# A two-layer GNN on one core: cell, picks and scatters streamed together, and a message stage with table offsets and types one group later

## The reference

```python
h = relu(layernorm(x))                                  # x: 12500 x 128
msg = h[src] @ W_msg.T + b_msg + edge_embed[type]       # 212500 edges, sorted by dst
m = segment_sum(msg, dst)                               # 12500 x 128
x = x + gru_cell(m, h, W_ih, W_hh, b_ih, b_hh)
h = relu(layernorm(x))
agg = segment_sum(h[dst], src)                          # layer 1: rows src, columns dst
z = ((1 + eps) * h + agg) @ W1.T + b1
z = relu(batchnorm(z, gamma, beta))                     # statistics over all nodes
x = x + z @ W2.T + b2
```

## Time and profile before

| what | value |
|---|---|
| runs | 5644.68, 5648.10, 5653.43 us; median 5648.1 us |
| profiled execution | 5650.5 us, its span 5648.7 us |
| mean granted TensorE clock | 0.644 |
| busy share of the span | PE 57%, PEld 46%, DVE 47%, ACT 28%, POOL 59% |
| DMA | 514 MB, 91 GB/s over the span |

### The profile page before, as it was taken

How to read it: one execution, slowest core, us unless ns; L and a number is a source line. 1 busy time by engine, 2 the same in 40 slices (tenths; PEclk the granted TensorE clock), 3 DMA queues, 4 the chain that set the end, 5 groups by cost and what they waited for, 6 DMA issues and landing times.

```text
span 5648.7 us, 78171 instructions
## 1 busy us (share of the span) xinstructions
PE 3221.0 (57%) x17495; PEld 2607.6 (46%) x17496; DVE 2670.9 (47%) x4799; ACT 1608.2 (28%) x3266; POOL 3336.2 (59%) x3510
## 2 busy tenths in 40 slices
PE   4566666666666665665943333333335666666767
PEld 3344444444444444444733222322324565556656
DVE  7566665666665656664641011111003444445557
ACT  4323222222222322222432222222222222221137
POOL 0666666666666666665136666666666666655563
PEclk8555555555555555555975555555556888878889
DMA  4222222222222111111222222222223444445455
GB/s 144 79 69 67 68 66 68 67 67 67 69 68 66 54 44 43 44 44 39 65 74 74 71 71 74 74 71 74 70 71 128 159 161 146 154 152 174 175 186 181
DMA packets 311629, 514.05 MB, mean 91 GB/s; under 512 B 68678, under 2 KB 227065, under 8 KB 295517
## 3 DMA queue, kind: packets, MB, share of 16 engines
q0 software_dynamic: 106944, 226.05, 13.4%
q1 hardware_dynamic: 118669, 242.40, 13.0%
q10 hardware_dynamic: 85904, 44.17, 2.6%
HBM read 331.72 MB, written 180.64 MB: 91 GB/s over the span
## 4 chain that ended last, share of the span: by engine, by line
another core or an unknown queue 33%; PE 25%; issue 20%; DVE 9%; ACT 5%; ACTq 2%; DVEq 2%; POOL 1%; DMA 1%; SPq 0%; POOLq 0%
PE ps L1700 6%; PE ps L1715 6%; PE ps L1569 4%; PE ps L1583 3%; PE ps L1591 2%; DVE sb_Y L1356 2%; ACT sb_counts L740 2%; DVE sb_blks L1157 2%; PE ps L1739 2%; ACT sb_ring L852 1%; ACTq L848 1%; PE ps L1712 1%; DVEq L1165 1%; DVE sb_oh L1146 1%
## 5 line engine op out<-in xcount | busy, mean ns | idle before, releaser
L649 POOL DMA_INDIRECT rows_by_src<-sb_ring,sb_posE x1664 | 1631.5, 980 | 966.1 <-ACT sb_ring L852 485.3
L626 POOL DMA_INDIRECT sb_ring<-msg_table,sb_stepE x1664 | 1576.9, 948 | 1034.6 <-SPq L466 498.6
L1700 PE MATMUL ps<-sb_H,sb_oh 128*128 x3520 | 725.0, 367 | 1161.9 <-issue 517.6
L1700 PEld LDWEIGHTS ps<-sb_H,sb_oh 128*128 128x128 f32 x3520 | 620.3, 263 | 1265.6 <-issue 1263.8
L1569 PE MATMUL ps<-sb_ring,sb_oh 128*128 x3520 | 926.9, 435 | 216.8 <-issue 208.4
L1569 PEld LDWEIGHTS ps<-sb_ring,sb_oh 128*128 128x128 f32 x3520 | 779.0, 319 | 310.0 <-issue 306.0
L1338 DVE TENSOR_SCALAR sb_oh<-sb_oh,sb_cf 128x512 f32<-128x512 bf16 x440 | 215.4, 503 | 1212.4 <-remote 933.9
L852 ACT COPY sb_ring<-ps 128x512 f32<-128x512 f32 x416 | 242.8, 584 | 1913.0 <-remote 1308.1
L740 ACT CAST sb_counts<-ps 54x512 bf16<-54x512 f32 x440 | 254.8, 579 | 1757.3 <-remote 1198.7
L1189 DVE TENSOR_TENSOR sb_Y<-sb_Y,ps 128x512 f32 x440 | 300.0, 682 | 636.6 <-remote 576.6
L1583 PE MATMUL ps<-sb_oh,sb_toh 128*54 128x128 bf16 x1760 | 320.0, 301 | 261.2 <-issue 252.3
(11 more groups left out here) (225 smaller groups left out, 3855.2 us busy)
## 6 DMA issues: line engine op xcount, KB each, us to landing
sb_stepE<-rows_by_src SPq DMA_DIRECT2D x114, 1088.0 KB
sb_oh<-step_targets SPq DMA_DIRECT2D x110, 512.0 KB
rows_by_src<-sb_cf ACTq DMA_DIRECT2D x294, 136.0 KB
sb_ring<-msg_table,sb_stepE POOLq DMA_INDIRECT x1664
rows_by_src<-sb_ring,sb_posE POOLq DMA_INDIRECT x1664
sb_ring<-rows_by_src SPq DMA_DIRECT2D x11, 1088.0 KB, 5.1
msg_table<-sb_oh SPq DMA_DIRECT2D x14, 448.0 KB, 3.2
sb_oh<-in_x SPq DMA_DIRECT2D x49, 128.0 KB, 2.1
```

The costliest lines, as they stand in the source:

```text
L626: pool.indirect_dma_start(out=ring[:, m % RGROUPS * G + q, 0:F], out_offset=None, in_=table_d[:, :], in_offset=bass.IndirectOffsetOnAxis(a ...
L649: pool.indirect_dma_start(out=rows_d[:, :], out_offset=bass.IndirectOffsetOnAxis(ap=posE[:, m * G + q:m * G + q + 1], axis=0), in_=ring[:, ...
L1700: m = mm(picked_ps[:, ds(slot, P)], pick[g][:, q * P:(q + 1) * P], H[:, ds(off, P)], start=False, stop=True, skip_group_check=True)
```

## The change

- Every block boundary gets a step without edges of its own: `STEPS` is 1856, `CHUNKS` 116, `GROUPS` 464; tiles and their number stay.
- Message stage: PE takes a step's place in its bank from a table row (`relrow`) instead of subtracting, and the number of tile groups needed from the same register (`wait_group`) instead of a load for each group. `add_types` of group n-1 stands behind the ranks of group n, and DVE's add too is one group later.
- The cell is unrolled; POOL's add moves to DVE; x1 goes to 8 small buffers, and ACT normalizes each turn's two blocks from there, with the deviations taken in 13 portions (`LN_ENDS`). Within the same turns the first 56 step groups (`STREAMED` = 7 pairs) are picked, copied and scattered, from turn 6 on. The separate stage of norms is gone.
- Picks use 2 banks instead of 4. A pick of group n waits until groups 0 to n-1 are copied and cleared (`bank_clear` >= n+2). ACT copies once per step group (464) to a place from a table (a spare place where no tile group ends) instead of once per tile group (416).
- POOL tells ACT which ring places are free (`ring_free`, after the DMAs of tile group m-2 have landed). SP relays `row_slot`. The DMAs that load rows for the sums and most of those for the targets are issued by ACT instead of SP.
- The compares of picks (after the streamed ones) and of sums read their constant from PSUM; a pick's `tensor_scalar` becomes a `tensor_tensor`.

```diff
-STEPS = E // P + BLOCKS
+STEPS = E // P + 2 * BLOCKS
+XB1, XSEMS = 8, 4
+LN_ENDS = (1, 3) + tuple(range(7, TURNS - 1, 4)) + (TURNS - 1,)
+STREAMED = -(-TURNS // (2 * GPC))
+SLOT_LAG = 2
...
+        def norm_lag(t):
+            return 6 if t < LN_ENDS[1] + 1 else 8
...
@@ POOL @@
             def scatter(m):
-                pool.wait_ge(S("row_moved"), m + 1)
+                if m >= SLOT_LAG:
+                    f = m - SLOT_LAG
+                    pool.wait_ge(S(f"ring_dma{f % RGROUPS}"), GATHERED + (f // RGROUPS + 1) * (G * 16))
+                    nc.gpsimd.sem_inc(S("ring_free"), G)
+                if m < AHEAD:
+                    pool.wait_ge(S("row_slot"), pool.value_load(endrow[:, m:m + 1], min_val=1, max_val=GROUPS))
+                else:
+                    pool.wait_ge(S("row_moved"), m - AHEAD + 1)
...
@@ ACT @@
+            def move_rows(n, g):
+                src = act.snap(place_regs[g], min_val=0, max_val=512)
+                dst = act.snap(place_regs[GPC + g], min_val=0, max_val=TRASH)
+                key = act.value_load(slot_keys[:, ds(n, 1)], min_val=1, max_val=TILES - G + 1)
+                rows = ring_steps[:, ds(dst, G * RW)].rearrange("p (q w) -> p q w", w=RW)
+                act.wait_ge(S("ring_free"), key)
+                nc.scalar.copy(rows[:, :, KEY:KEY + 1], key_cols[:, ds(key, G)].unsqueeze(2))
+                act.wait_ge(S("picked"), n + 1)
+                nc.scalar.copy(rows[:, :, 0:F], picks_f[:, ds(src, 512)].rearrange("p (q f) -> p q f", f=F)) \
+                    .then_inc(S("row_slot"), 1)
+                act.wait_ge(S("row_slot"), n + 1)
+                nc.scalar.copy(picks_f[:, ds(src, 512)], zeros_b[:, :]).then_inc(S("bank_clear"), 1)
...
+            for i in range(streamed + 10):
+                for n in (n for n in range(streamed) if n + norm_lag(n) + 2 == i):
+                    move_rows(n, n % GPC)
+                if i < TURNS:
+                    gates(i)
+                if i + 2 < TURNS:
+                    move_msg(i + 2)
+                if 1 <= i <= TURNS:
+                    candidate(i - 1)
+                if i - 4 in LN_ENDS:
+                    deviation1(i - 4)
+                for t in (t for t in range(TURNS) if t + norm_lag(t) == i):
+                    norm1(t)
...
@@ DVE @@
             step_blocks(first_d, bstep_d, blktmp)
+            step_blocks(first_m1, bnext_d, blktmp)
...
                         dve.wait_ge(S("y_zero"), 1)
-                    dve.wait_ge(S("agg_done"), n + 1)
-                    wait(dve, "agg_added", n)
-                    yb = Y[:, ds(offs[g], 512)]
-                    vs.tensor_tensor(yb, yb, bank(1 + g), ALU.add).then_inc(S("agg_added"), 1)
+                    else:
+                        add_group(n - 1, (g - 1) % G, off_sets[k if g else 1 - k][(g - 1) % G])
...
+            def stream(i):
...
+                if blend:
+                    dve.wait_ge(S("zhn_ready"), i)
+                    vs.tensor_tensor(hnbuf[o], hnbuf[o], nbuf[o], ALU.add).then_inc(S("hn_ready"), 1)
+                for n in (n for n in range(2 * GPC * STREAMED) if n + norm_lag(n) == i):
+                    layer1_pick(n // (2 * GPC), n // GPC % 2, n % GPC)
...
+                o = vs.tensor_scalar(pick[g], codes, row, None, ALU.is_equal) if row is iota_p \
+                    else vs.tensor_tensor(pick[g], codes, row.to_broadcast([P, 512]), ALU.is_equal)
...
-                                 iota_f.unsqueeze(1).to_broadcast([P, G, P]), ALU.is_equal).then_inc(S("key_oh_v"), 1)
+                                 key_iota.unsqueeze(1).to_broadcast([P, G, P]), ALU.is_equal).then_inc(S("key_oh_v"), 1)
...
@@ PE @@
+            def wait_group(g):
+                pe.reg_alu(need, regs[g * G], 1, ALU.max)
+                pe.wait_ge(S("tiles_in"), pe.snap(need, min_val=1, max_val=TGROUPS))
...
-                    o = bank(1 + g)[:, 0:P] if q == 0 else ps[:, 1 + g, ds(rel(g, q), P)]
+                    o = bank(1 + g)[:, 0:P] if q == 0 else ps[:, 1 + g, ds(place(s), P)]
...
+                    if not isinstance(n, int) or n > 0:
+                        add_types((g - 1) % G, n - 1)
                     pe.wait_ge(S("agg_zero"), n + 1)
-                    wait_tiles("tiles_in", n)
+                    wait_group(g)
                     sum_rows(g, k, n)
-                    add_types(g, n)
...
+            picked_ps = ps[:, 6:8, :].rearrange("p a b -> p (a b)")
+            def pick_group(n, g):
+                pe.wait_ge(S("bank_clear"), n + 2)
+                pe.wait_ge(S("pick_oh"), n + 1)
+                for q in range(G):
+                    off = pe.snap(regs[g * G + q], min_val=0, max_val=(BLOCKS - 1) * P)
+                    slot = pe.snap(slots[g * G + q], min_val=0, max_val=(2 * G - 1) * P)
+                    m = mm(picked_ps[:, ds(slot, P)], pick[g][:, q * P:(q + 1) * P], H[:, ds(off, P)],
+                           start=False, stop=True, skip_group_check=True)
+                m.then_inc(S("picked"), 1)
+            for i in range(streamed + 9):
+                if i < TURNS:
+                    gates(i)
+                if i + 2 < TURNS:
+                    msgT(i + 2)
+                if 2 <= i < TURNS + 2:
+                    back(i - 2)
+                for n in (n for n in range(streamed) if n + norm_lag(n) + 1 == i):
+                    pe.wait_ge(S("h2_norm"), min(n + 1, TURNS))
+                    pick_group(n, n % GPC)
```

More of the change, by code:

```diff
@@ L550, in _, with relay_rows @@
-            pick_loop(sp, feed)
+            for i in range(TURNS):
+                x1_out(i)
+                if i + 2 < TURNS:
+                    cell_in(i + 2, i % 2)
+                if i % GPC == 2 and i >= 10:
+                    c = (i - 10) // GPC
+                    sp.wait_ge(S("pick_oh"), (c + 1) * GPC)
+                    loc_in(sp, c + 2, c % 2)
+            def relay_rows(m, r):
+                last = sp.value_load(endrow[:, ds(m, 1)], min_val=1, max_val=GROUPS + 1)
+                sp.wait_ge(S("row_slot"), last)
+                nc.sync.sem_inc(S("row_moved"), 1)
@@ new lines, in norm1 @@
+            def norm1(i):
+                act.wait_ge(S("ln_ready"), sum(i > e for e in LN_ENDS) + 1)
+                for b in range(NG):
+                    n = i * NG + b
+                    o = nc.scalar.activation(H[:, n * P:(n + 1) * P], x1buf[i % XB1][:, b * P:(b + 1) * P], ACT.Relu,
+                                             bias=nbn[:, n:n + 1], scale=rstdn[:, n:n + 1])
+                o.then_inc(S("h2_norm"), 1)
+            place_regs = [act.alloc_register(f"slot_place{q}") for q in range(2 * GPC)]
@@ L857, in _ @@
-            act.wait_ge(S("ring_tails"), 1)
-            for g in range(GPC):
-                clear_picks(g).then_inc(S("bank_clear"), 1)
-            for r in range(RGROUPS):
-                move_rows(0, r)
-            with act.Fori(1, TGROUPS // RGROUPS) as j:
-                for r in range(RGROUPS):
-                    move_rows(j, r)
+                move_msg(k)
+            for g in range(2):
+                nc.scalar.copy(bank(6 + g), zeros_b[:, :]).then_inc(S("bank_clear"), 1)
+            streamed = 2 * GPC * STREAMED
@@ new lines, in _, with srows_in, slots_and_feed @@
+            act.wait_ge(S("x1_kept"), TURNS)
+            def srows_in(s, k):
+                act.dma_start(srows[k].rearrange("p a w -> p (a w)"), rows_of(s)) \
+                    .then_inc(S(f"rows_in{k}"), 16)
+            def slots_and_feed(j, k, sums, first, own):
+                c = j * 2 + k
+                if first in FIRST_C:
+                    z = FIRST_C.index(first)
+                    landed(act, z)
+                    for s, h in ((first, first % 2), (first + 1, 1 - first % 2)):
+                        wait(act, "sum_done", (s - 1) * GPC)
+                        srows_in(s, h)
+                slot_regs(c)
+                for g in range(GPC):
+                    move_rows(c * GPC + g, g)
+                    if g == GPC - 1 and not (isinstance(c, int) and c + 2 >= CHUNKS):
+                        loc_in(act, c + 2, k)
+                    for i, (s, h) in enumerate(sums):
+                        if (i * GPC + GPC - 1) // len(sums) == g:
+                            after = [FIRST_C[z + 1] for z in range(NPASS - 1) if isinstance(s, int) and s < FIRST_C[z + 1]]
+                            if not (isinstance(s, int) and s + 2 >= after[0]):
+                                act.wait_ge(S("sum_done"), (s + 1) * GPC)
+                                srows_in(s + 2, h)
@@ L1313, in norm_relu @@
[L1313 to L1325 removed]
+                        m = vs.bn_aggr(v[:, 2 * b:2 * b + 2], stats[:, b * 6:(b + 1) * 6])
```

484 lines of the change are left out of this document (246 added, 238 removed).

## The result

The kernel after takes 5733.15 us (median of 3 runs, 5730.66 to 5743.51) against 5648.1: ratio 1.0162, 95% interval 1.0145 to 1.0178. It is slower; the forecast was 5480 us.

What follows compares the result with a forecast made beforehand. No engine was taken as saturated: stages wait, with the ledger on POOL's queue. Terms 4 - 70 - 163 + 60 = -169 took 5650.5 to 5481 profiled, so 5480 us; range 5280 to 5740.

Steps and rivals of the forecast that it cites:

- the scatters' term: Scatters on POOL's queue: 2627 us against 2567, +60, with waits of 48 in streamed turns and 485 in later picks.
- and the old 1.6 with sums, where PE's sums fill the time: Picks with sums: POOL's wait per tile group stays at 1.6 us, 264 us in all.
- The message term: Message stage: PE's shorter work lets 2.5 step groups finish per ring refill, 186 waits, -70 us.
- next late is DVE: Message stage: PE's wait for ACT's copy goes; DVE, whose ranks PE needs, is late next. No size given.
- The bound of +27: Message stage, slow end: still 2.04 step groups per refill, 227 waits of 2.31 us, 525 us, +27.
- The gap: Between last gather and first scatter: 233.3 us falls to 70, -163.
- Streamed turns: Cell turns that also pick and scatter: 5.4 us each, 56 turns, 302 us for 50 tile groups.
- Rival A: Picks and streamed turns: held PE increments make the kernel slower, 5845 us at worst; chance 0.23.
- Constants in PSUM: Compares reading constants from PSUM shorten POOL's indirect DMAs: half of the 35 us excess, -18.
- 5740 with two of the three: Total if two of three prices hold: message 97, streamed turns +118, picks without sums +150.
- a drained POOL ends each hold, so waits limit themselves: Argument against the held-increments rival: late increments arrive once POOL has run dry. No size given.
- B: Whole kernel: POOL becomes the bound and the ring never runs dry, 5040 us, likelier 5260; chance 0.17.

Runs made afterwards that it cites:

- e8b: Repeat of the kernel after with four pick banks behind the streamed groups, early types and constants in SBUF; late (slower) chip: 5578.8 us, ratio 1.0002 to the kernel before.
- a2: The kernel after, unchanged, on a late (slower) chip: 5654.2 us, ratio 1.0133 to the kernel before.
- e6: The kernel after with types and adds back in their own step group, table offsets kept; late (slower) chip: 5647.3 us, ratio 1.0115 to the kernel before.
- e7: Both kernels with a lag between PE's picks and ACT's copy; late (slower) chips: before 5635.1 and 5626.0 us, after 5745.4 and 5752.0.
- e2: The kernel after with the compares' constants back in SBUF, on a prompt (faster) chip: 4739.0 us, ratio 0.9896 to the kernel before.
- e5: The kernel before with scatters as direct writes of a tile to a fixed place; late (slower) chip: 5018.7 us, one run.
- e8: The kernel after with four pick banks behind the streamed groups, early types and constants in SBUF; late (slower) chip: 5583.0 us, ratio 0.9994 to the kernel before.
- e3c: The kernel before with a pick waiting as if there were two banks, one tile group allowed uncopied; late (slower) chip: 5603.1 us, ratio 1.003.
- e1: The kernel before with only the order changed, types and adds one group later; prompt (faster) chip: 4789.5 us, ratio 0.9998.
- a0: The kernel after, unchanged, on a prompt (faster) chip: 4716.1 us, ratio 0.9848 to the kernel before.

## Why the prediction was wrong

- **The failed step: the scatters' term (+60, measured +225).** POOL's own time came out at 1614.6 + 463.9 us, 15 under the forecast's 2094. The waits are the error: 714 us against 48 + 485. By the waits in the three windows: streamed turns 107 us, forecast 48; without sums 244, forecast 221; with sums 364, forecast 264. More than half of the excess of 181 lies where the chain got no price, and the step that failed in words was "and the old 1.6 with sums, where PE's sums fill the time". It was 364/165 = 2.2 us per tile group there, since the strict chain runs beside the sums too (with slack behind the picks, e8b, POOL's waits for copies there were 299 us against 343 in a2); without sums, where I had priced the chain, 244/201 = 1.2 against 1.1.
- **The message term (-70, measured +27).** The wait for ACT's counts went and "next late is DVE" came true (L350's 422 us for L1275), but the term rested on PE's shorter work filling the ring faster, and that step failed too, by 97 us: POOL was refilled once in 464/209 = 2.2 groups, not 2.5, and waited longer each time (2.50 us for 2.31). The bound of +27 was hit to the microsecond, though by luck: it was reckoned from added groups, and in e6 and e7 these cost nothing and the later types about 27. On prompt chips there is no wait to win (2085 and 2086 us).
- **The gap (-163, measured -179)** had its reason right, on either kind of chip (-165): the first copy came 33 us after the cell's start, forecast 36. The rest is mostly an earlier start, 19 us after the last gather instead of 33.5.
- **Streamed turns (302 us, measured 367).** On a prompt chip they take 316 (5.6 us per turn), and the late increments add 51. The 5.4 was 4.6 of summed work and 0.8 for held increments. A prompt chip has no holds and still needs 5.6, so the sum of ACT's and POOL's times was 1.0 too low and the price came near by luck. Rival A's 7.5 us a turn was too much.
- **Constants in PSUM (-18).** POOL's scatters fell from 1631.5 to 1614.6 us, -17, but the half that I took was luck. The excess of mean over median went from 21 to 1 ns, nearly all of the 35 us and not half of it. The median rose from 959 to 969 ns, 17 us, for a reason that no run shows; e2 has the 969 too. And the 690 ns that the prediction sets beside what is said of PSUM operands belong to a compare that reads SBUF alone (L1346), so they don't show it; a pick's compare with an operand in PSUM takes 684 (L1428) where it took 503.
- **Rivals.** A had the mechanism and the sign, with 0.23 against the forecast's 0.45. That "5740 with two of the three" lies by the measured 5733 is partly luck: its message price came in full (97), of the streamed turns' 118 only 65, of the 150 without sums 23, and 100 came with sums, where A had no price. I weighed it down by "a drained POOL ends each hold, so waits limit themselves". The timeline of a2 has a hold that ends while POOL sends, and a chain that needs one increment of PE per step group pays one hold after another. B, POOL as the bound, is what a prompt chip shows for both kernels, before and after; with it the change is worth -70, not the -608 of B's 5040, as the gap closes by 165 and the scatters give 93 back.
- **What I had and didn't use.** The earlier trace rows showed a chain of late increments with no cause in the kernel. A forecast that rests on a state whose cause is unknown should have put more weight on the case in which it stays, and asked how much slack each kernel has against it: three uncopied tile groups allowed before when a pick starts, none after.

What is shown and what isn't: shown are the dependence on the chip or on something else that stayed the same within each of the six sets, the dependence on indirect DMAs (e5, one execution), that an equal lag costs the changed kernel more (e7), and that slack behind the pick takes the loss back (e8, e8b). Not shown is how the gain with sums divides between e8's edits; how much of the loss is the strict wait and how much the 464 copies instead of 416, as no run puts the strict wait into the kernel before (e3c's is looser by a tile group); and what differs in the chips.

## What to carry to other kernels

Before a chain of engines is tightened, ask what slack it had against a late signal: a ring or a set of banks that looks idle in the mean may carry the tail. Read in the waits whether a stage's releasers have names; "remote" in quantity, with two engines going on in the same instant, was in these runs a delay that other chips didn't have, so such a kernel should be measured on a second chip before a change is judged. And report such a change by chip: this one is 1.5% faster on one kind and 1.3 to 1.6% slower on the other.

## What the runs showed of the hardware

- The same kernel takes 4788 to 4792 us on three chips and 5576 to 5648 on others, with a granted clock about equal (0.65 and 0.64). Nearly the whole difference (833 of 862 us of span, e1 against the kernel before) lies in the stages with indirect DMAs: gathers 2086 against 2518 us, scatters 2166 against 2567.
- On the slower kind, ACT and DVE go on late when they wait for TensorE while GpSimd's indirect DMAs stream (954.7 us of "remote" in ACT's 171 waits for counts in 1900 us), and at once when GpSimd's DMAs are direct (none in 490 us of the same execution, e5).
- An indirect DMA of 128 rows costs POOL 947 to 998 ns in the mean and a pause of 0.305 us (median) on both kinds. On the prompt kind this is the whole pace of the gathers: 1.253 us x 1664 = 2085.
- A GpSimd direct DMA of one tile took 551 ns (e5, 3310 to 3800 us).
- VectorE's compares with all operands in SBUF lengthen the indirect DMAs beside them: 1019 ns in the mean with sums (e2), 968 with one operand in PSUM (a0).
